# A gated graph layer on one core: set-up with a wait for each load, first rows in pieces, the last stage's first loads inside the edge loop, and halves in the last stage

## What is computed

```python
pre_u = einsum('bud,dk->buk', h, W1[:d])
pre_v = einsum('bvd,dk->bvk', h, W1[d:])
hidden = relu(pre_u[:, :, None, :] + pre_v[:, None, :, :] + b1)
S = sigmoid(einsum('buvk,ko->buvo', hidden, W2)[..., 0] + b2[0])
a = einsum('buv,bud->bvd', S * adj, h)
m = einsum('uv,bud->bvd', adj, h) * h
z = beta1 * h + beta2 * (a @ Wa + ba) + beta3 * (m @ Wm + bm)
```

## Time and profile before

| | us |
|---|---|
| median of 3 runs | 3654.01 (3653.74 to 3662.95) |
| profiled execution, its own time | 3660.8 |
| span of the profiled execution | 3659.0 |
| TensorE busy | 3409.4 (93%) |
| VectorE busy | 2720.7 (74%) |
| ScalarE busy | 2335.8 (64%) |
| GpSimd busy | 1734.5 (47%) |
| mean granted TensorE clock | 0.976 |

### The profile page before, as it was taken

How to read it: one execution, slowest core, us unless ns; L and a number is a source line. 1 busy time by engine, 2 the same in 40 slices (tenths; PEclk the granted TensorE clock), 3 DMA queues, 4 the chain that set the end, 5 groups by cost and what they waited for, 6 DMA issues and landing times. The chain is left out here.

```text
span 3659.0 us, 56051 instructions
## 1 busy us (share of the span) xinstructions
PE 3409.4 (93%) x14232; PEld 2632.6 (72%) x14232; DVE 2720.7 (74%) x4866; ACT 2335.8 (64%) x14066; POOL 1734.5 (47%) x2306
## 2 busy tenths in 40 slices
PE   3999999999897899999999999999999999589998
PEld 2666565666565688878788888888888887478887
DVE  3555555655544799999999999999999999354444
ACT  0211211121111699989999999999999998578786
POOL 1211111211110556666666666566766665466664
PEclk9999999999998999999999999999999999789999
DMA  5666666666657866567666676666756653967674
GB/s 194 247 218 228 239 219 243 238 232 236 227 198 194 193 153 144 141 156 169 154 146 139 150 182 164 156 149 144 175 143 155 153 130 75 321 223 245 217 245 165
DMA packets 342570, 685.80 MB, mean 187 GB/s; under 512 B 38718, under 2 KB 252840, under 8 KB 319400
## 3 DMA queue, kind: packets, MB, share of 16 engines
q1 hardware_dynamic: 286704, 587.95, 56.2%
q0 software_dynamic: 21504, 53.31, 4.8%
q10 hardware_dynamic: 34032, 40.90, 3.2%
HBM read 444.01 MB, written 256.18 MB: 191 GB/s over the span
## 5 line engine op out<-in xcount | busy, mean ns | idle before, releaser
L1194 ACT ACTIVATE junk<-psum_a 128x128 f32<-128x128 f32 x6144 | 1606.7, 292 | 218.3 <-PE psum_a L1098 144.1
L1194 ACT ACTIVATION_READ_ACCUMULATOR junk<-psum_a 128x1 f32 x6144 | 1366.1, 223 | 0.0
L1139 DVE TENSOR_REDUCE group_sum<-psum_d 128x56 f32<-128x896 f32 x1024 | 1113.2, 1087 | 83.6 <-PE psum_d L1098 41.8
L1098 PE MATMUL psum_d<-v_t,pk 128*128 128x512 f32 x1920 | 754.6, 393 | 0.0
L1243 POOL DMA_INDIRECT sum_dram<-total,idx_all x512 | 505.9, 988 | 228.1 <-POOL total L1254 124.1
L1513 PE MATMUL z_psum<-hWa_all,masked 128*128 128x256 f32 x2048 | 471.3, 395 | 73.2 <-DVE masked L1497 48.1
L1097 PE MATMUL psum_d<-first_u,pk 128*128 128x512 f32 x1280 | 508.6, 397 | 23.6 <-DMA pk<-pick_dram 10.6
L971 POOL TENSOR_TENSOR own<-whole 128x256 f32<-128x256 f32 x128 | 113.0, 883 | 874.5 <-DVE own_mixed L769 537.3
L1097 PE MATMUL psum_d<-u_t,pk 128*128 128x512 f32 x1280 | 503.8, 394 | 13.1 <-issue 11.9
L727 ACT COPY whole<-ring 128x258 f32<-128x258 f32 x128 | 47.9, 374 | 723.5 <-PE ring L641 709.2
L1513 PEld LDWEIGHTS z_psum<-hWa_all,masked 128*128 128x128 f32 x2048 | 406.6, 199 | 137.9 <-issue 50.3
(11 more groups left out here) (213 smaller groups left out, 5098.5 us busy)
## 6 DMA issues: line engine op xcount, KB each, us to landing
sum_dram<-zero SPq DMA_DIRECT2D x128, 512.0 KB, 4.0
rows_dram<-split SPq DMA_DIRECT2D x128, 512.0 KB, 3.2
pk<-pick_dram SPq DMA_DIRECT2D x512, 128.0 KB
u_t<-rows_dram SPq DMA_DIRECT2D x64, 1024.0 KB
raw<-sum_dram SPq DMA_DIRECT2D x64, 1024.0 KB, 5.0
first_u<-rows_dram SPq DMA_DIRECT2D x62, 1024.0 KB
whole_dram<-whole SPq DMA_DIRECT2D x128, 256.0 KB, 3.4
pick_dram<-first_v SPq DMA_DIRECT2D x128, 256.0 KB, 3.4
```

What stands on the lines that cost most here:

```text
L1098: return nc.tensor.matmul(dst, pk[n % PKS][:, SLOTS + at:SLOTS + at + P], part(v_t[n % VG][:], b, LB), start=False, stop=True)
L1139: nc.vector.tensor_reduce(out_[:, :, 1:EG], in_[:, :, GW:LATE].rearrange("p b (g k) -> p b g k", k=GW), AX, ALU.add, apply_absolute_value= ...
L1194: last = nc.scalar.activation(junk[:, a % RING_A, k * LATE:(k + 1) * LATE], psum_a[a % RING_A][:, k * LATE:(k + 1) * LATE], ACT.Abs, accum ...
```

## The change

It does the following, and nothing else of the kernel's order changes.

- **Set-up is one step.** Each engine waits for its own load. SyncE loads W2, W1, h[0], b1, the adjacency and h[1] in this order; ScalarE's queue loads Wa, Wm, the biases and the betas. W1's copy goes to ScalarE, and so does half of `W1_k`'s. The transposes of h[0] and their copies move from the row stage into set-up. b1's product has 128 equal columns (`b1_wide`) in place of one and a copy over partitions. Of the chain on W2, the operations that the order does not need stand behind it. GpSimd clears the buffers.
- **Zeros.** No store of zeros stands in set-up; each of the first 16 tiles stores two.
- **Ring product.** Both linear columns stand in the half for v, so the half for u has 256 columns in place of 258.
- **First rows.** They are loaded in eight pieces, behind each tile of batch 15, four transfers of 64 rows x 512 each, and wait only for one tile's rows to have landed. Block 0's pick is loaded at the start of batch 15, into `places`.
- **Edge loop.** SyncE loads picks and v tiles in turn. GpSimd clears the gather buffers, and the first gather and its adds come three blocks later. At block 248 (`AHEAD`) SyncE waits for the left pairs, and for the sums up to eight blocks before, and loads the last stage's first two `raw` and `hWa`. The buffer `shared` holds in turn the adjacency with `hT` and `mT`, the gathered rows, and these four tiles. `of_u` is scaled at the end of this loop.
- **Last stage.** `of_v` is loaded in halves into three half buffers by SyncE; the first half of the next column is loaded at tile 3 and the second at tile 1 of that column. GpSimd adds in two halves (over v), VectorE masks in two halves (over batches) and ScalarE signals after each 8 batches; TensorE waits for each half. The sigmoid's table is touched once ahead. The last store is made in four quarters. If the further passes run, the two sums are loaded again.

Core of the diff:

```diff
+shared = sb("shared", [P, 3 * ROW])
+places = sb("places", [P, 2 * SLOTS], fp32r, scope=work)
...
-ZROWS, ZEARLY = N * N * B // (P * 1024), 16
+ZROWS, ZEARLY = N * N * B // (P * 1024), 2 * NT
...
         @block.sync
         def _(sp):
+            sp.dma_start(w2_all[:], W2.rearrange("k a -> a k").broadcast_to([P, D])).then_inc(w2_loaded, 16)
+            for w in range(2):
+                sp.dma_start(W1_sb[:, :, w, :], W1[w * D:(w + 1) * D, :].rearrange("(c p) k -> p c k", p=P)).then_inc(W1_loaded, 16)
+            sp.dma_start(h[0][:], x[0, :, :].rearrange("(t p) d -> p t d", p=P)).then_inc(h_loaded[0], 16)
...
-            sp.wait_ge(zero_set, 1)
-            for z_ in range(ZEARLY):
-                sp.dma_start(sum_fill[z_, :, :], zero[:]).then_inc(zero_stored, 16)
-            sp.wait_ge(loaded, n)
...
-        def load_first(i, b, end):
-            at, to = b * D, end * D
+        def load_first(i):
+            at, to = 2 * i * D, (2 * i + 2) * D
             for q in range(HALVES):
                 sp.dma_start(first_u[q * UB:(q + 1) * UB, at:to].bitcast(fp32),
-                             rows_dram[0:UB, 0, q, at:to]).then_inc(first_loaded[i], 16)
+                             rows_dram[0:UB, 0, q, at:to]).then_inc(first_loaded[2 * i // NT], 16)
                 sp.dma_start(first_v[q * VB:(q + 1) * VB, at:to].bitcast(fp32),
-                             rows_dram[0:VB, 1, q, at:to]).then_inc(first_loaded[i], 16)
+                             rows_dram[0:VB, 1, q, at:to]).then_inc(first_loaded[2 * i // NT], 16)
...
             if b == B - 1:
-                rows_landed(b * NT)
...
-                load_first(0, 0, B - 1)
+                for q in range(HALVES):
+                    sp.dma_start(places[q * VB:(q + 1) * VB, :].bitcast(fp32),
+                                 pick_dram[block_of(0, 0), :, :]).then_inc(pick_loaded[0], 16)
             for t in range(NT):
                 store_rows(b, t)
...
-                if b * NT + t + ZEARLY < ZROWS:
-                    sp.dma_start(sum_fill[b * NT + t + ZEARLY, :, :], zero[:]).then_inc(zero_stored, 16)
-            if b == B - 1:
-                rows_landed(B * NT)
-                load_first(1, B - 1, B)
+                if b == B - 1:
+                    row_landed((b if t == NT - 1 else b - 1) * NT)
+                    load_first(t)
+                g = b * NT + t
+                for z_ in ((2 * g, 2 * g + 1) if g < ZEARLY else (g + ZEARLY,)):
+                    if z_ < ZROWS:
+                        sp.dma_start(sum_fill[z_, :, :], zero[:]).then_inc(zero_stored, 16)
...
-                        last = nc.tensor.matmul(ring[:, w * BANK:w * BANK + CW], hT[:, c, s * P:(s + 1) * P], W1_k[:, c, w, :],
+                        cols = (D, CW)[w]
+                        last = nc.tensor.matmul(ring[:, w * BANK:w * BANK + cols], hT[:, c, s * P:(s + 1) * P], W1_k[:, c, w, 0:cols],
...
+AHEAD = n_blk - 8
+raw = [shared[:, 2 * ROW + i * P * B:2 * ROW + (i + 1) * P * B].rearrange("p (v b) -> p v b", b=B) for i in range(RAW)]
+hWa_ahead = [shared[:, i * ROW:(i + 1) * ROW].rearrange("p (b d) -> p b d", d=D) for i in range(RAW)]
...
-        load_pick(0)
         for n in range(1, PKS - 1):
             load_pick(n)
-        for jj in range(1, VG):
-            load_v(0, jj)
+            if n < VG:
+                load_v(0, n)
...
-                load_of_v(sp, 0)
+                for i in range(2):
+                    load_of_v(sp, i, of_v[:, i * HV:(i + 1) * HV, :])
+            if n == AHEAD:
+                sp.wait_ge(left_added, LEFT)
+                sp.wait_ge(left_d, LD * LEFT)
+                sp.wait_ge(left_a, LA * LEFT)
+                sp.wait_ge(left_scattered, 16 * (LEFT - 2))
+                for i in range(RING_S):
+                    sp.wait_ge(scattered[i], 16 * TILES * ((AHEAD - 8 - i + RING_S - 1) // RING_S))
+                for t in range(RAW):
+                    sp.dma_start(raw[t], sum_uv[t * P:(t + 1) * P, 0:P, :]).then_inc(raw_loaded[t], 16)
+                    sp.dma_start(hWa_ahead[t], hWa_dram[:, t * P:(t + 1) * P, :].rearrange("b p d -> p b d")).then_inc(hWa_loaded[t], 16)
...
-        for rows_ in (*left_rows, left_cols):
-            nc.vector.memset(rows_[:], 0.0).then_inc(left_set, 1)
...
+        for rows_ in (*left_rows, left_cols):
+            nc.gpsimd.memset(rows_, 0.0).then_inc(left_set, 1)
...
-                if step == 1:
+                late_by = 0 if w else 3
+                if step == 1 + late_by:
                     waits(pool, left_d, LD * (w - 1))
                     waits(pool, left_a, LA * (w - 1))
                     gather(w)
-                if 5 <= step < 9:
-                    add(w, step - 5)
+                if 5 + late_by <= step < 9 + late_by:
+                    add(w, step - 5 - late_by)
...
+of_vs = [of_v[:, 0:HV, :], of_v[:, HV:P, :], sb("of_v_next", [P, HV, B], scope=phase)[:]]
...
-                waits(sp, raw_added, k - RAW + 1)
-                sp.dma_start(raw[k % RAW][:], sum_uv[t * P:(t + 1) * P, vt * P:(vt + 1) * P, :]).then_inc(raw_loaded[k % RAW], 16)
-                waits(sp, gate_masked, k - ADJ + 1)
+                if t == 1 and vt:
+                    sp.wait_ge(raw_added, 2 * (k - RAW) + 1)
+                    load_of_v(sp, 2 * vt + 1, of_vs[(2 * vt + 1) % 3])
+                if k >= RAW:
+                    sp.wait_ge(raw_added, 2 * (k - RAW + 1))
+                if t == 3 and vt + 1 < NT:
+                    load_of_v(sp, 2 * vt + 2, of_vs[(2 * vt + 2) % 3])
+                if k >= RAW:
+                    sp.dma_start(raw[k % RAW], sum_uv[t * P:(t + 1) * P, vt * P:(vt + 1) * P, :]).then_inc(raw_loaded[k % RAW], 16)
+                waits(sp, gate_masked, MASKS * (k - ADJ + 1))
...
         for vt in range(NT):
-            pool.wait_ge(of_v_loaded, 16 * (vt + 1))
             for t in range(NT):
                 k = vt * NT + t
                 pool.wait_ge(raw_loaded[k % RAW], 16 * (k // RAW + 1))
                 step_done(pool, k - GM)
-                nc.gpsimd.tensor_tensor(masked[k % GM][:].rearrange("p b v -> p v b"), raw[k % RAW][:], of_v[:], ALU.add).then_inc(raw_added, 1)
+                for m in range(2):
+                    pool.wait_ge(of_v_loaded[m], 16 * (vt + 1))
+                    some = slice(m * HV, (m + 1) * HV)
+                    nc.gpsimd.tensor_tensor(masked[k % GM][:, :, some].rearrange("p b v -> p v b"), raw[k % RAW][:, some, :],
+                                            of_vs[(2 * vt + m) % 3], ALU.add).then_inc(raw_added, 1)
...
+                for m in range(MASKS):
+                    rows_ = masked[k % GM][:, m * HB:(m + 1) * HB, :]
+                    dve.wait_ge(gate_made, MASKS * k + m + 1)
+                    nc.vector.tensor_tensor(rows_, rows_,
+                                            adj_b[k % ADJ][:].rearrange("p (a v) -> p a v", a=1).broadcast_to([P, HB, P]),
+                                            ALU.mult).then_inc(gate_masked, 1)
...
+        nc.scalar.activation(warm[:], half_sign[:, 0:1], ACT.Sigmoid)
-                if t == NT - 1 and vt + 1 < NT:
-                    load_of_v(act, vt + 1)
...
+        for q in range(4):
+            act.wait_ge(z_ready, (B // 2) * (NT - 1) + 2 * (q + 1))
+            act.dma_start(out[4 * q:4 * q + 4, (NT - 1) * P:NT * P, :].rearrange("b p d -> p b d"),
+                          z[:, 4 * q:4 * q + 4, :]).then_inc(z_stored, 16)
```

373 lines of the change are left out of this document (196 added, 177 removed).

## The result

The changed kernel takes 3537.74 us (median of 4 runs, 3535.99 to 3539.98), the kernel before 3657.01 beside it (3653.74 to 3662.95). The ratio is 0.9678, with a 95% interval of 0.966 to 0.9695: faster by 119 us. The forecast was 131, to 3523. The profiled execution took 3539.98 (span 3537.9, clock 0.987), 121.1 less span than the one of before.

A forecast was written before the change was run, and what follows sets the result against it. TensorE was taken to bound the row stage and edge loop, DMA the edge loop's opening and the last stage's first column. Terms 48 + 1 - 2 + 8 + 16 + 24 + 32 + 4 = 131 us off 3654.0 gave 3523, range 3503 to 3552.

The forecast's parts named there:

- Set-up: Start of the kernel: without the zero stores the first ring product moves from 76.01 to 28.0 us, gaining 48 (43 to 51).
- TensorE: this is the late one: Set-up: of three racing chains, TensorE's transposes of h[0] end last, ready at 17.0 us against VectorE's 15.2.
- Zeros: Row stage's first two batches: the zero stores moved there fit beside other transfers, with a loss of 2 us (0 to 10).
- the ring product: Row stage: its first half loses 2 of 258 columns over 128 tiles, gaining 1 us.
- Batch 15: End of row stage: first rows in pieces end the stall behind four long transfers, gaining 8 us (4 to 9).
- The rival of pieces in series: Batch 15: pieces of first rows cost a fixed time each, 9.2 us a tile, 32 lost: 3555 us; chance 0.04.
- The opening: Edge loop's start: block 4, waiting for its u tile, starts at 1216 in place of 1232.20, gaining 16 us (8 to 18).
- The last stage's opening: Last stage up to block 8: fewer bytes ahead, products at about 3199 in place of 3223.12, gaining 24 us (16 to 29).
- Column ends: Last stage after block 8: of_v ahead saves 37 us, less 5 for the halves, gaining 32 (17 to 38).
- The rival of engines that shut each other out: Last stage: GpSimd adds and VectorE masks block each other, 7.2 us a tile, 18 lost: 3536 us; chance 0.10.
- The slow rival: Last stage: GpSimd's half add costs as much as the whole, 11.5 us a tile: 3801 us, slower; chance 0.02.
- Tail: End of the kernel: a quarter of the last store should land in half the time, gaining 4 us (2 to 5).

The follow-up runs named there:

- the zeros alone: Kernel before with only the 16 stores of zeros moved from set-up to the first 16 tiles, two pieces each: 3632.44 us against 3650.07, ratio 0.9942.
- column 0 finished early: Changed kernel, but VectorE adds column 0's sums to z ahead of block 8's mask, not behind it: 3533.95 us against 3537.74.
- the first rows whole: Changed kernel with first rows of batches 0 to 14 again in four transfers ahead of batch 15's stores, no pieces behind tiles: 3549.42 us against 3537.74.
- the gather at once: Changed kernel with the edge loop's first gather at block 1, as before, in place of block 4: 3555.18 us against 3537.74.
- whole masks: Changed kernel with VectorE's mask and ScalarE's signal for all 16 batches of a tile at once, GpSimd's adds still in halves: 3540.79 us against 3537.74.

## Why the prediction was right, and where it was off

The time lay in the range, and the likeliest case was the one that came: every seam gained, none turned. The sum was 10 us too high (131 against 121.1), from six terms that missed by 3 to 10 us and partly cancelled, so it is in part luck that the time came out within 15 us of the forecast. Both sides of the table are single traces. Some figures of the prediction do not come out as written, though none moves the forecast by more than 2 us: 3191 and 6.7 make 3198, not 3199; 56 x 0.3 is 17, not 18; 3880 less 72 is 3808, not 3801; and the pieces' 3555 lies outside a range that is said to reach it.

- **Set-up, 48 forecast, 43.7 measured.** Shown. "TensorE: this is the late one" failed: VectorE was, by 0.4 us (20.32 against 19.95). Its chain took 10.7 us of its own (10.9 forecast), but the first operation was held 3.4 us by GpSimd's clear, which the prediction did not see. W2's load landed at 6.2, just past its bounds, and that cost nothing, since the operation ended with the clears wherever it began. h[0] landed at 14.9, not 12.5. From the order to the products 3.56 us (3.4 forecast), and the products up to b1's end 7.45 in place of 6.6. That the stores' issue was more than half of the gain is shown by the zeros alone.
- **Zeros, -2, and the ring product, +1.** Batches 0 and 1 take 57.3 us and lead by 43.8 at their end: no cost. The 5.9 us lost behind them are not shown to come of the change. From batch 1's product with Wa to batch 14's it is 906.9 us before and 909.4 with the zeros moved, and 912.9 in the changed kernel; the eleven others with its row stage up to there take 907.8 to 914.6. Two things make up this scatter. One is TensorE's idle time (66.8 us against 62.2 before), nearly all of it behind VectorE's work on the picks; VectorE waits for a pick's buffer to be stored, 117.9 us in 36 waits before and 130.8 in 38 after, up to 1040 us. The other is the granted clock: the kernel with column 0 finished early has the same waits (130.7 in 38, TensorE idle 66.2) and takes 907.8, and the difference is in TensorE's busy time, 841.6 against 846.1, with 17.1 us at the lower level against 23.9. What sets either was not tried by itself.
- **Batch 15, 8 forecast, 8.8 measured.** Shown by the first rows whole. The rival of pieces in series is out: a piece of 128 KB took 3.2 us to land (median of 32), and tiles are still 5.2 us apart.
- **The opening, 16 forecast, 12.8 measured.** That block 4's u tile decides was right, and so was the sum's form (a u tile is two transfers of 1024 KB, 2 MiB, and not the 4 that the description of the edge loop gives; the sum has 2); 10.2 MB took 50.6 us from the first load, 202 GB/s and not 219. What the prediction did not price apart is now shown: with the gather at once block 4 comes 14 us later. More than all of the 12.8 comes from the edits, since the trace of before has the shorter of the two old openings (83.8 and 90.4 us).
- **The rest of the edge loop, nothing forecast, 4.8 measured.** From block 4 to the last u tile's load it is 1816.5 us before and 1811.7 in the changed kernel. These are the two ends of what the fourteen traces show: the eleven other variants of the changed kernel take 1812.2 to 1815.8, the zeros alone 1814.8. Of the 4.8 us, 3.6 are TensorE's busy time (1811.2 against 1807.6) and 1.6 its wait at block 52, where a v tile and a u tile are loaded together (2.82 us against 1.20; at most 2.95 in the others). Scatter, and not tried by itself.
- **The last stage's opening, 24 forecast, 14.3 measured.** The bytes were nearly right: block 8's sum landed 73.1 us behind the first load, 70.8 forecast. The step that failed is "GpSimd's second half 2.4 and half of ScalarE's 6.2 and half a mask 1.2", 6.7 us. It took 15.4: both halves of the add (5.7), as the halves are over nodes and ScalarE's batches need all nodes; all of ScalarE's 6.3; the second mask half at 2.7; and then a sum to z. The last link is shown by finishing column 0 early.
- **Column ends, 32 forecast, 37.8 measured.** The 37 of the working was within 1 us, and the 5 taken off for the halves did not exist: the steady tile takes 6.907 us. The rival of engines that shut each other out is right in its mechanism (a half mask has 1210 ns at least and 3380 in the middle, a half add 2354 and 2932), but its price, 7.2 us a tile, did not come. The least durations alone, 2 x 2.35 + 2 x 1.21 = 7.13, are over the 6.907 that were held from block 9 to the end, while a tile's adds ended 13.9 to 15.7 us ahead of its products throughout. With whole masks the same tile of 6.907 us holds two adds of 2.35 and a mask of 2.29 at the least, 6.99, and 7.16 by the medians (2377 and 2409 ns). So not all of a mask and an add keep each other out. The Trainium skill's rule (SBUF — State Buffer, Summary: rules for kernel authors: for two SBUF inputs against a GpSimd operation that reads SBUF, the second blocks fully) would have made 7.13 the least; here the measurement decides. That the time of 3537.74 lies nearer to this rival's 3536 than to the forecast is chance: the 18 us that it expected this stretch to lose were not lost. The slow rival needed 9.2 us a tile and is out.
- **Tail, 4 forecast, 4.7 measured.** From the last product's end to the end of the span it is 8.7 us before and 4.0 after. The store in quarters was not tried by itself, and neither was the early touch of the sigmoid's table.

## What to carry to other kernels

Price a seam by the last link of its chain: of the four edits at the edge loop's opening, moving one 4 MB gather behind the transfer that decides was worth 14 us up to there, the other three together no more than the traces scatter. When work is cut in halves, ask along which axis each engine cuts; a half over nodes does not start an engine that wants all nodes. A clear that is moved to idle GpSimd is free only if it does not run beside a short chain on VectorE. And ask what two traces of one kernel differ by before a difference of 5 us in a long stretch is explained.
